# A graph and expert kernel: side work in fewer steps of the edge stage, narrower count windows, z rows loaded three steps ahead

## The reference

```python
h = x @ W
deg = segment_sum(ones, dst_f); dinv = rsqrt(deg)          # dst_f, src_f: the edges and one self loop a node
norm = dinv[src_f] * dinv[dst_f]
out = segment_sum(h[src_f] * norm[:, None], dst_f) + conv_bias
...
x = x + gnn(xn) + mix(xn)                                   # mix: attention, rmsnorm, + xn
x = x + ffn(layernorm(x))                                   # 8 experts, top 2
```

## Time and profile before

| | |
|---|---|
| median of the runs | 1396.51 us (3 runs: 1396.51, 4098.23, 1393.88) |
| the profiled execution | 1399.66 us, its span 1397.8 us |
| edge stage (142 us to the last add) | to 806.7 us |
| busy over the span | TensorE 89%, VectorE 70%, GpSimd 62%, ScalarE 38% |
| experts, the last stage | TensorE's products make up most of the chain that ended last |

### The profile page before, as it was taken

The page is one execution under the profiler, slowest core; times in us unless marked ns, Lnnn a source line. Parts: engine busy times, 40 slices in busy tenths (PEclk is TensorE's granted clock), DMA queues, the critical chain, the costliest instruction groups (busy, mean ns, idle before and its releaser), DMA issues. The chain is left out here.

```text
span 1397.8 us, 30557 instructions
## 1 busy us (share of the span) xinstructions
PE 1249.0 (89%) x8314; PEld 1116.5 (80%) x8315; DVE 976.5 (70%) x2903; ACT 531.0 (38%) x1417; POOL 870.2 (62%) x850
## 2 busy tenths in 40 slices
PE   5997788888888999999888887994799999999998
PEld 4983777777778888988777776883699999999997
DVE  8997777777778888887876467998544444444444
ACT  7706300221113333333322200446455555555553
POOL 1393777777777777777776500441377766666665
PEclk9999799999999999999989998995699999999999
DMA  7005333333356666777888800349444444444443
GB/s 241 0 0 184 113 103 106 104 105 106 117 172 173 178 205 203 213 221 224 268 256 265 264 5 1 116 127 311 119 68 70 68 69 73 67 72 72 68 68 44
DMA packets 132084, 183.07 MB, mean 131 GB/s; under 512 B 20988, under 2 KB 109768, under 8 KB 131856
## 3 DMA queue, kind: packets, MB, share of 16 engines
q0 software_dynamic: 44400, 92.92, 28.6%
q1 hardware_dynamic: 87584, 89.00, 20.0%
HBM read 149.38 MB, written 33.41 MB: 131 GB/s over the span
## 5 line engine op out<-in xcount | busy, mean ns | idle before, releaser
L731 POOL DMA_INDIRECT RG<-table,srci x504 | 494.6, 981 | 161.9 <-issue 156.0
L748 PEld LDWEIGHTS ps<-S_t,RG 128*128 128x128 f32 x2016 | 274.2, 198 | 60.7 <-DMA RG<-table,srci 45.9
L748 PE MATMUL ps<-S_t,RG 128*128 128x96 f32 x2016 | 284.8, 281 | 38.9 <-DMA RG<-table,srci 36.4
L1991 POOL DMA_INDIRECT out<-R,S_t x105 | 166.3, 1584 | 99.2 <-DVE R L1961 58.8
L770 PE MATMUL ps<-zrow,R 128*128 128x256 f32 x686 | 199.0, 396 | 17.0 <-DMA zrow<-table 8.9
L1002 DVE TENSOR_TENSOR R<-R,ps 128x392 f32 x280 | 156.6, 559 | 76.6 <-PE ps L758 56.1
L1874 PE MATMUL ps<-R,RG 128*128 128x128 f32 x1680 | 207.2, 277 | 0.0
L1884 PE MATMUL ps<-R 128*128 x840 | 198.5, 379 | 0.0
L1874 PEld LDWEIGHTS ps<-R,RG 128*128 128x128 f32 x1680 | 198.3, 194 | 0.3 <-issue 0.3
L1907 ACT ACTIVATE R<-ps,RG 128x128 f32<-128x128 f32 x420 | 120.1, 368 | 175.7 <-PE ps L1874 175.7
L1957 DVE TENSOR_TENSOR R<-ps,R 128x256 f32<-128x256 f32 x105 | 44.6, 424 | 201.5 <-PE ps L1884 201.5
(11 more groups left out here) (359 smaller groups left out, 1993.9 us busy)
## 6 DMA issues: line engine op xcount, KB each, us to landing
zrow<-table SPq DMA_DIRECT2D x336, 128.0 KB
RG<-table,srci POOLq DMA_INDIRECT x504, 3.1
ntable<-R SPq DMA_DIRECT2D x12, 516.0 KB
table<-RG SPq DMA_DIRECT2D x12, 512.0 KB, 2.9
out<-R SPq DMA_DIRECT2D x12, 512.0 KB, 3.1
R<-in_x SPq DMA_DIRECT2D x6, 896.0 KB
R<-in_w SPq DMA_DIRECT2D x8, 514.0 KB, 6.9
slot<-in_x SPq DMA_DIRECT2D x32, 128.0 KB
```

Of the source, the lines that this page charges most:

```text
L731: nc.gpsimd.indirect_dma_start(out=grows[:, s, :], out_offset=None, in_=table, in_offset=bass.IndirectOffsetOnAxis(ap=srci[:, ND + q, c:c ...
L748: last = nc.tensor.matmul(window(q % 2)[:, h, :], grows[:, s, h * P:(h + 1) * P], S_t[:, q % 2, c, :], start=c == 0, stop=c == GC - 1)
L1991: nc.gpsimd.indirect_dma_start(out=a_out, out_offset=bass.IndirectOffsetOnAxis(ap=sct[:, t:t + 1], axis=0), in_=yr[:, t % 4, :], in_offset ...
```

## The change

- The side stages get other steps: keys 0 to 12 (before 16), context 14 to 35 (18 to 45), queries 38 to 92 (48 to 100), residual 95 to 124 (102 to 124). Tables are built and used earlier, and the last is used up at step 117 instead of 125.
- The count windows are 5, 5, 6, 7, 8, 8, 8 nodes for the seven blocks instead of 8: counts, keys and chunk adds have 245, 294, 343 or 392 columns. The limits that set the flag follow.
- z rows get eight slots instead of six, the two more being the first two slots of the x ring, which idle until the residual begins. From product 200 on (EARLY) there are six again.
- SP loads z rows three steps ahead instead of two, x tiles two as before. Tiles 0 and 1 wait for product 200 to be over.

```diff
-DW = 8
+DWB = (5, 5, 6, 7, 8, 8, 8)
+DW = max(DWB)
...
-                nc.vector.tensor_scalar(slowT[:, 0:ND, :], dstrel[:, 0:ND, :], float(DW), -1e6, ALU.is_lt, ALU.mult)
+                for g0, g1, d in RUNS:
+                    nc.vector.tensor_scalar(slowT[:, g0:g1, :], dstrel[:, g0:g1, :], float(d), -1e6, ALU.is_lt, ALU.mult)
...
-        A0, A1 = 0, 16
-        C0, C1 = 18, 45
-        B0, B1 = 48, 100
-        D0, D1 = 102, GQ - 2
-        BUILT = (0, 45, 63, 76, 88, 98, 108, 116)
-        USED = (45, 63, 76, 88, 98, 108, 116, GQ - 1)
+        A0, A1 = 0, 12
+        C0, C1 = 14, 35
+        B0, B1 = 38, 92
+        D0, D1 = 95, GQ - 2
+        BUILT = (0, 35, 50, 64, 77, 90, 100, 109)
+        USED = (35, 50, 64, 77, 90, 100, 109, 117)
...
+        EARLY = sum(1 for q in range(D0 - 4) for _ in products(q))
+        ZW = ZR + 2
+        place_of, turn_of, ahead_of, held_by = {}, {}, {}, {}
+        for i in PROD:
+            k = i % (ZW if i < EARLY else ZR)
+            place_of[i], ahead_of[i] = k, held_by.get(k, (None, 0))[0]
+            held_by[k] = (i, held_by.get(k, (None, 0))[1] + 1)
+            turn_of[i] = held_by[k][1]
...
-                    if i >= ZR:
-                        sp.wait_ge(z_used, i - ZR + 1)
+                    if ahead_of[i] is not None:
+                        sp.wait_ge(z_used, ahead_of[i] + 1)
+                    elif place_of[i] >= ZR:
+                        sp.wait_ge(key_ok, 1)
...
                     if t >= XR:
                         sp.wait_ge(res_ok, t - XR + 1)
+                    elif t < 2:
+                        sp.wait_ge(z_used, EARLY)
...
-                for q in range(-2, GQ - 2):
-                    for b, j in products(q + 2):
+                for q in range(-3, GQ - 2):
+                    for b, j in products(q + 3):
                         z_rows(b, j)
                     for t in share(q + 2, D0, D1, T):
                         x_tile(t)
...
-                    nc.tensor.matmul(psK[m % 2][:, 0:T * DW], hots[m % 4], hotk[m % 4], start=True,
+                    wide = T * DWB[block_of(m)]
+                    nc.tensor.matmul(psK[m % 2][:, 0:wide], hots[m % 4], hotk[m % 4][:, 0:wide], start=True,
                                      stop=True).then_inc(cnt_ps, 1)
```

More of the change, by code:

```diff
@@ L30 @@
 NDB = len(DBLK)
-DW = 8
+DWB = (5, 5, 6, 7, 8, 8, 8)
+DW = max(DWB)
 DLIM = P - DW
 MD = ND * GC
+RUNS = [(min(g0 for (g0, _), k in zip(DBLK, DWB) if k == d), max(g1 for (_, g1), k in zip(DBLK, DWB) if k == d), d)
+        for d in sorted(set(DWB))]
+assert all((d - 1) * -(-WIN // d) < WIN for d in DWB) and list(DWB) == sorted(DWB) and T * DW <= 512
 GQ = NG - ND
@@ L360, in _ @@
                                              base=ND, pattern=[[0, 1]], channel_multiplier=-1))
-                step(nc.gpsimd.affine_select(out=isd[:, 1:2], in_=ones[:, 0:1], compare_op=ALU.is_ge, fill=float(WIN // DW),
-                                             base=-ND, pattern=[[0, 1]], channel_multiplier=1))
                 pool.sem_inc(const, 1)
+                step(nc.gpsimd.memset(isd[:, 1:2], 1.0))
+                for _, g1, d in reversed(RUNS):
+                    step(nc.gpsimd.affine_select(out=isd[:, 1:2], in_=isd[:, 1:2], compare_op=ALU.is_ge,
+                                                 fill=float(-(-WIN // d)), base=-g1, pattern=[[0, 1]], channel_multiplier=1))
                 step(nc.gpsimd.iota(iwin_i, pattern=[[1, P]], base=0, channel_multiplier=0))
@@ L639, in products, with z_slot @@
                     yield b, j
+        PROD = [b * T + j for q in range(GQ) for b, j in products(q)]
+        EARLY = sum(1 for q in range(D0 - 4) for _ in products(q))
[6 more added lines that the diff above has]
+            turn_of[i] = held_by[k][1]
+        assert PROD == list(range(NDB * T))
+        def z_slot(i):
+            k = place_of[i]
+            return zrow[:, k, :] if k < ZR else slot[:, k - ZR, :]
         def block_rows(b):
@@ L656, in build @@
             clear = semaphore(phase, "a_counts_cleared")
-            z_in = [semaphore(phase, f"a_z_rows{k}") for k in range(ZR)]
+            z_in = [semaphore(phase, f"a_z_rows{k}") for k in range(ZW)]
             z_used = semaphore(phase, "a_z_rows_used")
@@ L769, in product @@
                     n = P if j < T - 1 else TAIL
[L770 removed]
+                    nc.tensor.matmul(psD[:, 0:D], adj[b % 2][0:n, j, :], z_slot(i)[0:n, :], start=j == 0,
                                      stop=j == T - 1).then_inc(z_used, 1)
@@ L1157, in _ @@
                 near = S_t[:, 1, :, :].rearrange("p c w -> p (c w)")[:, 0:MD]
-                ch.done(nc.vector.tensor_scalar(near, key, float(DW), None, ALU.is_lt))
-                ch.done(nc.vector.scalar_tensor_tensor(key, high, float(DW), key, ALU.mult, ALU.add))
+                for g0, g1, d in RUNS:
+                    some = slice(g0 * GC, g1 * GC)
+                    last = nc.vector.tensor_scalar(near[:, some], key[:, some], float(d), None, ALU.is_lt)
+                ch.done(last)
+                for g0, g1, d in RUNS:
+                    some = slice(g0 * GC, g1 * GC)
+                    last = nc.vector.scalar_tensor_tensor(key[:, some], high[:, some], float(d), key[:, some], ALU.mult,
+                                                          ALU.add)
+                ch.done(last)
                 ch.done(nc.vector.scalar_tensor_tensor(key, key, 1.0, near, ALU.add, ALU.mult))
```

13 lines of the change are left out of this document (8 added, 5 removed).

## The result

The changed kernel takes **1422.55 us** (median of 4 runs, 1421.25 to 1425.38), the kernel before 1395.36 us beside it (1393.88, 1394.21, 1396.51 and one execution of 4098.23 us, which nothing here explains and which the ratio leaves out): ratio **1.0199, 95% interval 1.018 to 1.0218**. It is slower, by 2.0%; whether by more than 2% or less, the interval does not tell. The profiled execution took 1422.27 us against 1399.66 before, with a span of 1420.5 us against 1397.8.

The account below looks back on a forecast made before the run. GpSimd's serial gathers were taken to bound the edge stage. Chained x tiles (135 + 13 us) and what follows end it at 834.5 us, +27.8; with preamble 0.5, 1428 profiled, less 3.15 for the median: 1425 us, range 1396 to 1456.

Parts of the forecast that it names:

- Pace of the gathers: Edge stage to step 95: GpSimd's gathers keep 5.10 us a step; denser side work costs nothing, at most 10 us.
- Narrower chunks, nothing on the path: VectorE's chunk adds in the edge stage: narrower columns save some 25 us, hidden behind the gathers, so no time gained.
- Preamble +0.5: Before the edge stage: more small steps for the table of limits and the degree loop cost 0 to 1.6 us, taken as 0.5.
- Leads: SP's queue: x tiles had mostly 0.75 step before; after, many wait for a product of VectorE's own quarter step or later.
- Start of the chain: Step 96: VectorE's residual add of x tile 1, where the loop of waits begins, put at 647 us.
- Length of the chain: Residual adds of tiles 1 to 33, steps 96 to 115: 13 hops 75 us, TensorE's program 60, low clock 13.
- Behind the chain: Edge stage's end after tile 33: 3.7 us to group 120, 24 gathers 30.5 us, tail 5.3, ending at 834.5 us.
- The other signs: Edge stage: x waits over 60 us, single ones 3 to 5, GpSimd waiting for TensorE, end past 820 us, lower clock.
- B: Rival, edge stage: x tiles chained, but TensorE's clock holds or landings are short; +15 us, 1412 us; chance 0.28.
- C: Rival: x tiles do not bind; slow gathers halve (-5 us), tail shrinks (-8 us), 1384 us; chance 0.15.
- D: Rival: TensorE becomes the bound in steps 14 to 35; at 6.3 us a step costs 10 us, 1394 us; chance 0.05.
- F: Rival: x tiles chained with all of TensorE's 60 us at 1.2 GHz; 47 us more than forecast, 1472 us; chance 0.05.

Follow-up runs that it names:

- run 9: The changed kernel with all seven count windows at their old width of 8: 1421.78 us, ratio 1.0198 to the kernel before.
- Run 11: The changed kernel with x tiles queued ahead of each turn's z rows and all count windows at the old width of 8: 1385.61 us, ratio 0.9928.
- run 2: The changed kernel with each turn's x tiles queued ahead of its z rows, z rows still three steps ahead: 1519.77 us on a slower chip, ratio 0.9919.
- run 6: The changed kernel with x tiles queued ahead of the turn's z rows, measured again on another slow chip: 1522.72 us, ratio 0.9931.
- run 10: The kernel before with each turn's x tiles queued ahead of its z rows, z rows two steps ahead: 1444.57 us, ratio 1.0345.
- run 12: The changed kernel with z rows two steps ahead again and x tiles queued ahead of them: 1397.65 us, ratio 1.0039.
- run 1: The changed kernel with z rows again two steps ahead, all else kept: 1520.65 us on a slower chip, ratio 0.9941.
- run 5: The changed kernel again, unchanged, on a chip where the kernel before takes 1533.5 us: 1548.67 us, ratio 1.0106.

## Why the prediction was right

It was right in direction, in size (1425 forecast, 1422.55 measured) and in mechanism; the single terms are less exact than the sum, and that they come out within 2.5 us is in part luck. The profiled execution was put at 1428 and took 1422.27, 5.7 us less: the stage ended 3.5 us earlier than forecast, with the preamble's 0.5 counted in, and the rest of the kernel took 2.1 less than before, where nothing was forecast. To get the median of the runs, 3.15 us were taken off, the distance in the kernel before. In the changed kernel the median lies 0.3 us above its profiled execution, and so 3.4 us of the miss went away by chance.

- **Pace of the gathers.** Said: 5.10 us a step to step 95. Group 96 starts at 628.9 us, so 5.07. Right. The denser side stages cost nothing there.
- **Narrower chunks, nothing on the path.** A chunk add of 464 ns on average saves 26.6 us of VectorE, where 25 were said, and run 9 shows that without them the time is the same (1.0198 against 1.0199). Run 11 (0.9928) against runs 2 and 6 (0.9919, 0.9931) shows it also where the chain is gone, though on different chips. Right.
- **Preamble +0.5.** The first gather starts at 142.4 us instead of 142.03. Right.
- **Leads.** The program gives the leads of the changed kernel as said. Of the kernel before it gives 0.75 to 1.5 steps for 46 of the 49 tiles, and 0.75 for 14 of them; "for most tiles 0.75" was too short, and nothing in the sum hangs on it.
- **Start of the chain.** The residual add of tile 1 was put at 647 us; it starts at 641.61: 5.4 us too late.
- **Length of the chain**, tile 1 to tile 33: said 75 + 60 + 13 = 148; measured 788.00 - 641.61 = 146.4 us. The landing of all x tiles has a median of 2.9 us (2.0 to 5.8), not 3.7. For the 13 tiles of the chain the timelines of SP and ScalarE give, from issue to the start of the scaling, 2.1 to 5.6 us, 44.2 in all and 3.4 on average, the longest at tile 33 (781.80 to 787.37 us). So the 13 hops are 71 us and not 75. The clock over 662 to 793 us is 0.84 where 0.82 was taken, 11 instead of 13. Some 64 us are left for what was put at 60, TensorE's own program between one-hots and gate. Errors of -4, -2 and +4 us have nearly cancelled. The bound of 4.9 us for a landing was too low: it holds for the tiles of the kernel before from 700 us on, over all its tiles the longest took 6.2.
- **Behind the chain.** From tile 33 to group 120: said 3.7, measured 794.83 - 788.00 = 6.8. The 24 gathers take 31.9 us (said 30.5), the tail 4.8 (5.3; the prediction's own rows, 269.85 to 275.36 us, give 5.5). The stage ends at 831.5, forecast 834.5.

```profile
641.61 0.43 DVE L1098 TENSOR_TENSOR R<-R,slot 128x256 f32<-128x256 f32 x1 [1.54 <-ACT slot L938]
...
788.00 0.43 DVE L1098 TENSOR_TENSOR R<-R,slot 128x256 f32<-128x256 f32 x1 [6.72 <-ACT slot L938]
```

```profile
794.83 0.94 POOL L758 DMA_INDIRECT RG<-table,srci  x1 [8.22 <-PE ps L775]
```

VectorE's timeline gives the first two, GpSimd's the third. At tile 33, the one with the worst lead (half a step), the wait is 6.72 us, and GpSimd stands still for 8.22 us behind it: longer than the single waits of 3 to 5 us that were foretold, since at the chain's end every engine has used up its lead.

TensorE was to idle 2.5 to 3.5 us in every hop; its waits for one-hots are 2.2 us on average.

The other signs came as said: x waits over 60 us (71.8), GpSimd waiting for TensorE (45.9 us in 11 waits, one such wait of 3.49 us before), a stage end past 820, a lower clock.

**The rivals.** B (the clock holds, or landings are short) falls in its first half: the clock is 0.78 to 0.92 in the stretches of the chain. Its second half came true in part, the landings being 4 us shorter in all, and the chain still took 146 us. C, the change at its best, is 1384 us; run 11, the changed kernel without the chain (with the wide windows, which cost nothing), takes 1385.61 beside a kernel before of 1394.03. Its stage ends at 793.7 us, 13.0 earlier than before, which is C's -5 and -8; 789.9 was put as the ceiling. The median is only 8.4 us under that of its kernel before and not C's 12.5. So the side stages' new steps give two thirds or more of what was worked out, and the order in one loop took 36 us back. D never showed. F (the chain all at the low clock) falls too. The stretches of 30 us are mixtures, as windows of 5 us show (columns as above):

```profile
705.00:710.00 5.00, 1.39 (x7) 1.36 (x7) 2.31 (x7) 1.20 (x2) 3.67 (x4) 0.84 0.75 245
710.00:715.00 5.00, 5.00 (x20) 4.44 (x19) 1.80 (x6) 0.00 (x0) 0.00 (x0) 0.50 0.40 114
715.00:720.00 5.00, 4.91 (x31) 4.30 (x30) 3.85 (x12) 1.20 (x2) 3.62 (x4) 0.98 0.64 191
```

TensorE works 1.39 us in the first window, the second is wholly at the lower level (0.50) though TensorE is full in it, and the third is nearly all at the higher one. The same fall follows two other gaps, to 0.50 from 730 and 0.52 from 765 us; in other turns, from 695 to 705 or from 770 to 785 us, the clock stays at 1.00. So the gaps hold it down for a part of some turns and not for the whole chain. The Trainium skill's "TensorE: Matmul & The Clock Gate", HAM oscillation, was cited for F. The trace agrees with it on the fall, and in some turns on the low start, but it doesn't show this in every turn: no stretch of 30 us or more in the chain is below 0.78.

**Where the reasoning was short** was behind the prediction. Of the x tiles only one side was counted: how late the load ahead of them is released. Their own gate, a residual add of VectorE, and who stands behind it weren't. By the program of run 10 the x tile's lead was 1.5 to 2.5 steps, and from this came an expectation of 0 to 1% faster; it was 3.45% slower, with the same loop running over the z rows. The cause is shown for run 10 by its waits and the timeline, for run 12 by its waits, and by run 11, which differs from run 12 in the z rows' step of lead (and in the width, worth nothing here) and has 8.1 us of z waits where run 12 has 39.9.

## What to carry to other kernels

- A queue that issues in order, with entries that wait for different engines, makes each entry wait for the gates of all that stand ahead. For every entry count two leads: from the latest gate at or ahead of it to its use, and the same for what stands behind it. A lead through zero on either side closes a loop over all engines, which costs 1.1 to 3.5% here, with no engine and no DMA full.
- Loading one kind further ahead is not free for the other kind: move both, or put the one with the short lead first and give the other the spare step. Two remedies that work alone can undo each other (runs 1, 2 and 12).

## What was not expected of the hardware

Chips differ much more than the 2% at issue. On two of them the kernel before takes 1530.02 and 1533.5 us, 10% more than on the others, steadily (1524.01 to 1533.13 in 15 runs on the first). A gather is no longer there, 949 ns at the median against 946, and in the first 142 us TensorE is busy for 109.2 us against 109.4. But in the edge stage all engines stand idle for reasons that the profile can't place. From 142 to 756 us of run 5 the waits have rows that don't exist on the other chips, or only as short ones (`remote` is a wait whose end the profile puts down to no instruction of this core):

```profile
POOL RG L758 <- remote: 93.2, 68, 3.1
...
ACT R L902 <- remote: 81.2, 23, 8.4
...
DVE R L1032 <- remote: 65.3, 38, 6.9
PEld ps L786 <- issue: 65.2, 36, 11.1
```

The first residual add of run 5 comes at 757.0 us, that of the changed kernel on the first chip at 637.0. The rest of the kernel behind the stage takes 589.8 us there against 589.0. So the 10% arise in this one stage, in which all engines work at once; what holds them isn't shown by these traces and was not tried. It also matters for the verdict: the same change is 2.0% slower on one chip and 1.1% on the other, and the kernels with one remedy are 0.5 to 0.8% faster than before on both kinds.

A second number of use: in the chain, where the DMA share is lower (0.65 against 0.88 in the second of the short stretches), a 128 KB x tile lands in 2.9 us at the median instead of 3.7. Run 12 lies between in both, with shares of 0.74, 0.70 and 0.92 from 662.3 to 762.6 us and a median of 3.4. That fewer loads compete is the likely reason; no run changes the load alone.
